# Routed experts: token rows carry their residual, number and weight, each expert scatters its finished rows to the output, and the row loads are cut into 96 and 11 partitions

## The chip, the cores and the metric

The kernel runs on one core of a Trainium2 chip. The metric is the device time of one execution in microseconds (us). A core has a matrix engine (TensorE, PE in the rows; its weight loads are PEld), a vector engine (VectorE, DVE), a scalar engine (ScalarE, ACT), GpSimd (POOL) and SyncE (SP), each with its own instruction stream. They meet through semaphores, and data moves between the chip's memory and the on-chip memory through 16 DMA engines. A DMA is issued by an instruction on some engine's queue; here SP issues the plain loads and stores, and POOL the indirect ones, whose row addresses come from a tile of indices.

## The reference

Six layers on 2048 tokens (32 batches of 64) of 256 values. The change touches the last one, a feed-forward layer with eight experts, and the end of the layer before it:

```python
capacity = int(N / E * 1.25) + 1            # 2048 / 8 * 1.25 + 1 = 321
logits = xf @ wg
scores = softmax(logits)
top1 = argmax(scores)                       # the expert of each token
combine_w = scores[top1]
rank = cumsum(one_hot(top1), axis=0)[top1] - 1
valid = rank < capacity
slot = where(valid, top1 * capacity + rank, trash)
buf = zeros(...).at[slot].set(xf)           # xf: the normalised tokens, by expert
h = gelu(buf[e] @ W1[e] + b1[e])            # 321 x 256 -> 321 x 1024
y = h @ W2[e] + b2[e]                       # -> 321 x 256
out = x + where(valid, y[slot], 0) * combine_w
```

Everything is float32.

## The kernel before, in words

`perceiver` calls six stages one after the other. Between two stages all engines meet at a barrier, and each stage has its own tiles and semaphores. The change is in the last two.

**The Laplacian attention and router** (`laplacian_attention_and_router`, line 2059) works on 8 groups of 256 tokens: two streams, four rounds of a loop. For each group SP loads the residual and the attention of the stage before (L2130, L2131), and stores `x4` (the residual that the expert layer adds to, L2141), `xn` (its layer norm, the experts' input, L2145) and the router's logits (L2149). SP issues what belongs to one group in the order in which it is made. Loads are issued one round ahead. The two groups' steps alternate by `in_turn`. The tile `b.y4` may be written again once the stores of the round before have landed, which DVE checks by the semaphore `out` against 48 r (three stores of 16 each). At the start of this stage POOL clears a zero tile (L2162), and when the first layer norm is done it stores zeros over the whole of `buf` with four DMAs (L2167). `buf` is 8 x 321 = 2568 rows of 256 values in the chip's memory, 321 rows for each expert.

**The routed experts** (`routed_experts`, line 2305) has these parts:

1. *Routing.* SP loads the logits, four constants, `xn` into the tile `xs` (L2375), the weights of experts 0 and 1 (L2361 to L2363: 1 MB, 1 MB and a bias row broadcast to 128 partitions), and `x4` into `x4s` (L2378). DVE computes each token's expert and rank (L2476 to L2512) and gives two index tiles: `put` (where the token's row goes in `buf`) and `get` (where its result will stand in `ybuf`). PE helps with two products for the counts (L2424, L2425).
2. *Scatter.* POOL waits for `xs` and the indices and writes the 2048 rows of `xn` to `buf` with 16 indirect DMAs of 128 rows (L2458).
3. *Experts.* SP waits until all 16 have landed, loads the rows of experts 0 and 1 into `xe` (L2381) and then issues the weights of experts 2 to 5 (six sets of weight buffers, `NW`). An expert's 321 rows stand on 107 partitions, three rows on each, so the load is a transfer of 107 partitions of 3072 B. `xe` has two buffers. In its loop SP waits until expert e has been transposed, loads the rows of e + 2 (L2389), waits for the result `ye` and stores it to `ybuf` (L2391, 107 partitions again), and then loads the weights of e + 6.
   PE does for each expert: six transposes of `xe` (L2433), wait for ScalarE's copy `xeT` (L2409), 16 products for the hidden layer (L2441; each shows as two records), wait for the last of the eight Gelus (L2414), and 24 products for the output (L2447). DVE adds the bias from PSUM into `ye` (L2521, L2522).
4. *Combining.* POOL waits until all of `ybuf` has landed (L2462) and reads the 2048 result rows back in token order with 16 indirect DMAs (L2464). DVE multiplies each by its weight and adds `x4s` (L2530), and SP stores the output in four DMAs of 512 tokens (L2398).

`rows_of(b, e)` (line 2355) gives the rows of expert e as 107 partitions of three rows. `Chain.step` makes DVE wait for its own instruction.

Of the kernel before, what the change touches and what calls it, by code (L numbers as in the profile page):

```python
# [20 lines left out]
TOK = 128  # L21
# [2028 lines left out]

ERF_P = (-2.72614225801306e-10, 2.77068142495902e-08, -2.10102402082508e-06, -5.69250639462346e-05,
# [7 lines left out]
def laplacian_attention_and_router(nc, consts, x2, oT, W, x4, xn, logits, buf):  # L2059
# [6 lines left out]
    E = W["wg"].shape[1]  # L2066
    with ExitStack() as ctx:
# [15 lines left out]
        zeros = m.sbuf("zeros", [ROWS, 6 * 256])  # L2083
# [42 lines left out]
        def _(sp):  # L2126
# [6 lines left out]
            def work(b, r, more):  # L2133
# [7 lines left out]
                sp.dma_start(tiles_of(x4, 2 * r + b.number), b.y4[:]).then_inc(b.sem("out"), 16)  # L2141
                yield
# [13 lines left out]
            for b in streams:  # L2156
                sp.wait_ge(b.sem("out"), 48 * R)

        @block.gpsimd
        def _(pool):  # L2160

            nc.gpsimd.memset(zeros[:], 0.0).then_inc(sem("zeros"), 1)  # L2162
            pool.wait_ge(sem("zeros"), 1)
            pool.wait_ge(streams[0].sem("a_norm"), 1)
            slots = buf.rearrange("(a p t) n -> a p (t n)", p=ROWS, t=6)
            for a in range(buf.shape[0] // (6 * ROWS)):
                pool.dma_start(slots[a], zeros[:]).then_inc(sem("zeroed"), 16)  # L2167
            pool.wait_ge(sem("zeroed"), 16 * (buf.shape[0] // (6 * ROWS)))

        @block.scalar  # L2170
        def _(act):
            act.wait_ge(sem("const_in"), NL)
            def work(b, r):
# [21 lines left out]
                act.wait_ge(b.sem("out"), 48 * r)  # L2195
# [44 lines left out]
        def _(dve):  # L2240
# [12 lines left out]
            def work(b, r):  # L2253
# [37 lines left out]
                dve.wait_ge(b.sem("out"), 48 * r)  # L2291
# [13 lines left out]
def routed_experts(nc, consts, x4, xn, logits, W, buf, ybuf, out):  # L2305
# [9 lines left out]
    FAR = 100000.0  # L2315
    NW = 6
    assert TE * ROWS == CAP
    with ExitStack() as ctx:
# [6 lines left out]
        xs = m.sbuf("xs", [TOK, NT, D])  # L2325
        x4s = m.sbuf("x4s", [TOK, NT, D])
# [14 lines left out]
        get = m.sbuf("get", [TOK, NT], U32)  # L2341
# [4 lines left out]
        xe = m.sbuf("xe", [ROWS, 2, TE, D])  # L2346
# [24 lines left out]
        def _(sp):  # L2371
            sp.dma_start(lg[:], logits.rearrange("(t p) e -> p t e", p=TOK)).then_inc(sem("lg_in"), 16)
            for dst, src in ((ident[:], consts["ident"]), (upto[:], consts["upto"]), (order[:], consts["order"]), (b1[:], W["b1"])):
# [22 lines left out]
            for t in range(0, NT, 4):  # L2396
                sp.wait_ge(sem("mix"), t // 4 + 1)
                sp.dma_start(out[TOK * t:TOK * t + 4 * TOK, :].rearrange("(t p) n -> p t n", p=TOK), x4s[:, t:t + 4]).then_inc(sem("out"), 16)  # L2398
            sp.wait_ge(sem("out"), 16 * (NT // 4))

        @block.scalar
        def _(act):
            act.wait_ge(sem("shifted"), 1)
            nc.scalar.activation(ex[:], ex[:], ACT.Exp).then_inc(sem("exp"), 1)
            act.wait_ge(sem("const_in"), 64)

            def expert(e, par):
                act.wait_ge(sem("xT_ps"), e + 1)
                nc.scalar.activation(xeT[:, par], pX[:, :, 0:CAP], ACT.Copy).then_inc(sem("xT"), 1)  # L2409
                if e:  # L2410
                    act.wait_ge(sem("y_ps"), e)
                for f in range(NFT):
                    act.wait_ge(sem("h_ps"), e * NFT + f + 1)
                    nc.scalar.activation(hT[:, f, :], pH[:, f % 4, 0:CAP], ACT.Gelu, bias=b1[:, bass.ds(e, 1), f:f + 1].rearrange("p a b -> p (a b)")).then_inc(sem("h"), 1)  # L2414
            for e in range(E):
                expert(e, e % 2)

        @block.tensor
        def _(pe):
            pe.wait_ge(sem("const_in"), 64)  # L2420
# [7 lines left out]
            def expert(e):  # L2428
                i, par, at = e // 2, e % 2, e % NW
                pe.wait_ge(sem(f"xe_in{par}"), 16 * (i + 1))  # L2430
                for k in range(2):
                    for t in range(TE):
                        o = nc.tensor.transpose(pX[:, k, ROWS * t:ROWS * t + ROWS], xe[:, par, t, 128 * k:128 * k + 128], ident[0:ROWS, 0:ROWS])  # L2433
                o.then_inc(sem("xT_ps"), 1)
                pe.wait_ge(sem("xT"), e + 1)
                weights_here(pe, e)
                for f in range(NFT):
# [4 lines left out]
                    o.then_inc(sem("h_ps"), 1)  # L2442
                pe.wait_ge(sem("h"), (e + 1) * NFT)
                pe.wait_ge(sem("ye"), e)
# [3 lines left out]
                o.then_inc(sem("y_ps"), 1)  # L2448
            for e in range(E):
# [3 lines left out]
        def _(pool):  # L2453
            nc.gpsimd.memset(ones[:], 1.0).then_inc(sem("set"), 1)
            pool.wait_ge(sem("xs_in"), 16)
            pool.wait_ge(sem("slots"), 1)
            for t in range(NT):
                pool.indirect_dma_start(buf, bass.IndirectOffsetOnAxis(put[:, t:t + 1], 0), xs[:, t, :], None,  # L2458
                                        bounds_check=SLOTS - 1, oob_is_err=False).then_inc(sem("put"), 16)
            pool.wait_ge(sem("put"), 16 * NT)  # L2460
            for par in range(2):
                pool.wait_ge(sem(f"ye_out{par}"), 8 * E)  # L2462
            for t in range(NT):
                pool.indirect_dma_start(xs[:, t, :], None, ybuf, bass.IndirectOffsetOnAxis(get[:, t:t + 1], 0),  # L2464
                                        bounds_check=SLOTS - 1, oob_is_err=False).then_inc(sem(f"got{t // 4}"), 16)

        @block.vector
        def _(dve):
# [5 lines left out]

            dve.wait_ge(sem("lg_in"), 16)
# [4 lines left out]
            dve.wait_ge(sem("const_in"), 64)  # L2480
# [27 lines left out]
            chain.step(v.tensor_scalar(get[:], slot[:], float(SLOTS - 1), None, ALU.min))  # L2508
            chain.step(v.tensor_tensor(weight[:], weight[:], room[:], ALU.mult))
# [5 lines left out]
            def expert(e):  # L2515
                i, par, at = e // 2, e % 2, e % NW
                dve.wait_ge(sem("y_ps"), e + 1)
                weights_here(dve, e)
                if i:
                    dve.wait_ge(sem(f"ye_out{par}"), 16 * i)  # L2520
                v.tensor_tensor(ye[:, par, 0:2], pY[0:ROWS, 0, :].rearrange("p (t n) -> p t n", n=D), b2[0:ROWS, at].unsqueeze(1).to_broadcast([ROWS, 2, D]), ALU.add)  # L2521
                v.tensor_tensor(ye[:, par, 2], pY[0:ROWS, 1, 0:D], b2[0:ROWS, at], ALU.add).then_inc(sem("ye"), 1)  # L2522
            for e in range(E):
                expert(e)

            dve.wait_ge(sem("x4_in"), 16)
# [21 lines left out]
def shape_constants(latents=64, experts=8, buckets=32):  # L2548
# [81 lines left out]
```

## Time and profile before

| | us |
|---|---|
| median of 3 runs | 3820.42 (3816.07 to 3820.52) |
| the profiled execution's own time | 3818.75 |
| its span in the trace | 3817.0 |
| PE busy in the span | 3019.8 (79%) |
| DVE busy | 2548.8 (67%) |
| ACT busy | 1931.1 (51%) |
| POOL busy | 748.6 (20%) |
| start of the Laplacian stage (its first load) | 3286.09 |
| start of the expert stage (its first load) | 3503.85 |

The profile is of one execution. Times of instructions are counted from the start of the span. A row of the timeline has the start, the duration, the engine, the line of the kernel and the operation with what it writes and reads; "x48" is the number of records merged into the row, and the brackets say how long the engine had been idle and what ended that. "PEclk" is the granted TensorE clock as a share of 2.4 GHz, so 0.50 is the lower level, 1.2 GHz. "DMA" is the mean busy share of the 16 DMA engines, so that one engine alone gives 0.06.

### The profile page before, as it was taken

To read this page: it belongs to the slowest core of one execution; us is meant where nothing else is said; L and a number is where in the kernel's file an instruction comes from. 1 tells how busy PE (TensorE), PEld (TensorE's weight loads), DVE (VectorE), ACT (ScalarE), POOL (GpSimd) and SP (SyncE) were. 2 spreads that over 40 slices of the span, in tenths; PEclk is the share of its full clock that TensorE was granted. 3 is DMA by queue.
4 is the path that set the end of the run, shared out by engine and by line. 5 is a ranking of instruction groups with operands and counts; after the bars stand their busy time and mean duration, and the time that the engine had idled before them with its cause. 6 is when DMAs were issued, how large, how long until landed. Compare 5 with 4: busy or idle time off the path is not lost. (4 is left out here: it accounts for less than half of the span.)

```text
span 3817.0 us, 103916 instructions
## 1 busy us (share of the span) xinstructions
PE 3019.8 (79%) x36990; PEld 2570.1 (67%) x36990; DVE 2548.8 (67%) x7485; ACT 1931.1 (51%) x4178; POOL 748.6 (20%) x836
## 2 busy tenths in 40 slices
PE   3449999999999985566379999999999999543674
PEld 3348888888888884444258788787888888432453
DVE  5568888888888854766567777776777777464000
ACT  1146666667666643333236666666666666321111
POOL 0223233332333310000132211211221221001001
PEclk7669999999999996777569999999999999765887
DMA  2123332323323302000111111111111111213411
GB/s 65 52 85 81 82 83 81 81 82 82 83 81 80 84 10 66 23 22 17 37 33 40 42 42 40 42 40 39 43 39 43 43 39 27 77 41 111 156 48 61
DMA packets 235455, 221.58 MB, mean 58 GB/s; under 512 B 69516, under 2 KB 228545, under 8 KB 234816
## 3 DMA queue, kind: packets, MB, share of 16 engines
q1 hardware_dynamic: 232896, 208.22, 19.4%
q0 software_dynamic: 2048, 6.68, 0.5%
q8 instruction: 304, 4.98, 0.5%
q14 instruction: 207, 1.70, 0.1%
HBM read 186.30 MB, written 28.39 MB: 56 GB/s over the span
## 5 line engine op out<-in xcount | busy, mean ns | idle before, releaser
L1867 ACT ACTIVATE xb_P<-xb_sc 124x1024 f32<-124x1024 f32 (+1 forms) x416 | 405.6, 1023 | 428.9 <-PE xb_sc L1959 428.9
L2029 DVE CUSTOM_DVE_ANT_0 xb_junk<-xb_ring,xb_mbias 128x372 bf16<-128x372 f32 (+2 forms) x1024 | 526.3, 571 | 102.9 <-PE xb_ring L1936 98.6
L1936 PE MATMUL xb_ring<-xb_khi,xb_qhi 32*128 32x372 f32 (+2 forms) x1024 | 405.5, 443 | 45.4 <-DVE xb_kf L2014 16.0
L879 PE MATMUL xa_acc<-xa_raw,xa_P 124*128 124x193 f32 x1664 | 315.6, 330 | 7.3 <-ACT xa_P L754 7.0
L1959 PE MATMUL xb_sc<-xb_qs,xb_kf 32*124 32x128 f32 x6656 | 317.3, 271 | 0.0
L2014 DVE COPY xb_kf<-xb_ring 128x372 f32<-128x372 f32 (+2 forms) x256 | 138.8, 572 | 244.8 <-ACT xb_khi L1831 239.8
L1907 PE MATMUL xb_ring<-xb_xst,xb_whi 128*128 128x372 f32 (+2 forms) x768 | 263.2, 370 | 43.6 <-DVE xb_xst L2008 38.0
L1907 PE MATMUL xb_ring<-xb_whi,xb_xst 128*124 128x256 f32 (+1 forms) x1248 | 286.4, 292 | 2.9 <-DVE xb_maxes L2029 0.4
L1936 PEld LDWEIGHTS xb_ring<-xb_khi,xb_qhi 32*128 32x128 f32 x1024 | 181.3, 185 | 153.1 <-DVE xb_maxes L2029 56.4
L1959 PEld LDWEIGHTS xb_sc<-xb_qs,xb_kf 32*124 32x124 f32 x6656 | 282.7, 182 | 0.0
L879 PEld LDWEIGHTS xa_acc<-xa_raw,xa_P 124*128 124x128 f32 x1664 | 266.4, 189 | 18.7 <-ACT xa_P L754 12.3
L1804 POOL TENSOR_SCALAR xb_augk<-xb_mask,xb_some 1x1602 bf16<-1x1602 uint8 x128 | 206.4, 1613 | 252.6 <-PE xb_sc L1959 236.0
L865 PE MATMUL xa_sc<-xa_qblk,xa_kT 128*124 128x128 f32 x1664 | 239.0, 272 | 0.0
L1976 PE MATMUL xb_acc<-xb_P,xb_val 124*17 124x64 f32 x13312 | 230.8, 220 | 4.2 <-ACT xb_P L1867 4.2
L1907 PEld LDWEIGHTS xb_ring<-xb_whi,xb_xst 128*124 128x124 f32 (+1 forms) x1248 | 216.8, 188 | 22.7 <-DVE xb_maxes L2029 15.9
L672 POOL CAST xa_kTr<-xa_kT 128x744 fp32r<-128x744 f32 (+1 forms) x128 | 109.9, 858 | 621.2 <-ACT xa_kT L740 621.2
L1976 PEld LDWEIGHTS xb_acc<-xb_P,xb_val 124*17 124x17 f32 x13312 | 190.7, 97 | 44.0 <-issue 15.7
L1907 PE MATMUL xb_ring<-xb_wlo,xb_xst 128*124 128x256 f32 (+1 forms) x832 | 218.3, 284 | 0.0
L865 PEld LDWEIGHTS xa_sc<-xa_qblk,xa_kT 128*124 128x124 f32 x1664 | 216.1, 187 | 0.1
L1956 PE MATMUL xb_sc<-xb_augq,xb_augk 32*124 32x256 bf16 (+1 forms) x1664 | 201.3, 303 | 1.6 <-ACT xb_P L1867 1.6
L1907 PEld LDWEIGHTS xb_ring<-xb_xst,xb_whi 128*128 128x128 f32 x768 | 146.5, 193 | 76.7 <-issue 43.0
L1907 PE MATMUL xb_ring<-xb_xst,xb_wlo 128*128 128x372 f32 (+2 forms) x512 | 180.2, 352 | 0.0
(430 smaller groups left out, 7720.8 us busy)
## 6 DMA issues: line engine op xcount, KB each, us to landing
xa_raw<-in_ctx SPq DMA_DIRECT2D x64, 279.0 KB
ex_w<-in_W SPq DMA_DIRECT2D x16, 1024.0 KB, 10.1
xa_raw<-in_ctx SPq DMA_DIRECT2D x32, 372.0 KB
xa_xTr<-in_ctxT SPq DMA_DIRECT2D x64, 186.0 KB, 2.5
xb_raw<-in_ctxT SPq DMA_DIRECT2D x64, 186.0 KB, 2.5
xa_xTr<-in_ctxT SPq DMA_DIRECT2D x32, 248.0 KB, 2.7
xb_raw<-in_ctxT SPq DMA_DIRECT2D x32, 248.0 KB
xa_mask<-in_mask SPq DMA_DIRECT2D x32, 200.1 KB, 5.3
```

The source lines that it names most:

```text
L672: nc.gpsimd.tensor_copy(kTr[:, c % 2, :, 0:W], kT[:, p, :, k0:k0 + W]).then_inc(sem("kTr"), 1)
L865: i = nc.tensor.matmul(s_[0:w, 256 * u + 128 * o:256 * u + 128 * o + 128], kt[:, o, :], qblk[:, t3, o, :], start=False, stop=True, skip_gr ...
L879: i = nc.tensor.matmul(acc[:, o, :], w, raw[0:KEYS, t3, t, :], start=t == 0 and o == 0, stop=t == NKT - 1, skip_group_check=True)
L1804: nc.gpsimd.tensor_scalar(augk[r:r + 1, p, :], mask8[r:r + 1, :], -1.0, some[r:r + 1, 1:2], ALU.add, ALU.mult).then_inc(sem("augk"), 1)
L1867: nc.scalar.activation(P[0:w, pbuf(t, p), :].rearrange("p (r n) -> p r n", r=4), sc[0:w, :, half], ACT.Exp).then_inc(sem("exped"), 1)
L1907: i = nc.tensor.matmul(out, l, r, start=k == 0, stop=k == 4)
L1936: i = nc.tensor.matmul(bank[:, 0:w], qhi[r, p, o, 128 * s:128 * s + 128], khi[r, p, o, k0:k0 + w], start=True, stop=True)
L1956: nc.tensor.matmul(sc[0:w, r, at:at + 256], augk[rows(r), p, keys], augq[rows(r), p, :], start=True, stop=True)
L1959: i = nc.tensor.matmul(sc[0:w, r, at + 128 * o:at + 128 * o + 128], kf[rows(r), p, o, keys], qs[rows(r), p, o, 128 * (r % 2):128 * (r % 2) ...
L1976: i = nc.tensor.matmul(acc[32 * j:32 * j + VW, 64 * g:64 * g + 64], val[0:w, p, c, h, :], P[0:w, pbuf(c, p), place(h):place(h) + 64], star ...
L2014: v.tensor_copy(kf[:, p, o, k0:k0 + w], ring[f % 3][:, 0:w]).then_inc(sem("kf"), 1)
L2029: v.tensor_tensor_reduce(out=junk[:, k, 0:w], in0=ring[f % 3][:, 0:w], in1=mbias[:, p, k0:k0 + w], scale=1.0, scalar=-3.0e38, op0=ALU.add, ...
```

## The change

In the Laplacian stage:

- `x4` of each group is stored a second time, to `out`. The semaphore is counted against 64 r.
- `buf` has rows of 528 values (2112 B): 256 of `xn`, 256 of `x4`, and 16 more of which two are used. It is cleared as a flat tensor with 9 DMAs of 128 partitions and 1177 values, from a tile of that size.

In the expert stage:

- One tile `row` (128 x 16 x 528) takes the place of `xs` and `x4s`. It is loaded in four DMAs: `xn` and `x4` for the first eight tiles of tokens, then for the last eight. DVE clears the last 16 columns, and puts in the token's number (from a new constant, counted from 1) and its weight.
- The scatter's first eight DMAs wait for the first half of `row`, the others for the second.
- `xe` has four buffers (`NX`) of 528 values a row. The load of an expert's rows is two DMAs, of partitions 0 to 95 and 96 to 106, now 6336 B on each partition. Four experts are loaded at once after the scatter; the rows of e + 4 are loaded when `ye` of expert e is done.
- PE transposes the rows of expert e + 1 (`turn`) between the hidden and the output products of expert e, and ScalarE copies them (`turned`) after the Gelus of e.
- After the bias, DVE makes the output's row numbers (`to`; a row without a token gets a number beyond the bound) and computes weight times result plus residual in three instructions. PE waits for `biased`, not for `ye`.
- POOL scatters the three rows of each partition to `out` with three indirect DMAs of 107 rows for each expert. `ybuf`, the read back, DVE's combining pass and the four stores are gone.

```diff
+EXTRA = 16
@@ laplacian_attention_and_router
+    SHARE = buf.shape[0] * buf.shape[1] // 128
+    SIZE = next(k for k in range(3000, 0, -1) if SHARE % k == 0)
-        zeros = m.sbuf("zeros", [ROWS, 6 * 256])
+        zeros = m.sbuf("zeros", [128, SIZE])
                 sp.dma_start(tiles_of(x4, 2 * r + b.number), b.y4[:]).then_inc(b.sem("out"), 16)
+                sp.dma_start(tiles_of(out, 2 * r + b.number), b.y4[:]).then_inc(b.sem("out"), 16)
-            slots = buf.rearrange("(a p t) n -> a p (t n)", p=ROWS, t=6)
-            for a in range(buf.shape[0] // (6 * ROWS)):
-                pool.dma_start(slots[a], zeros[:]).then_inc(sem("zeroed"), 16)
+            flat = buf.rearrange("s n -> (s n)").rearrange("(p q) -> p q", p=128)
+            for k in range(0, SHARE, SIZE):
+                pool.dma_start(flat[:, k:k + SIZE], zeros[:]).then_inc(sem("zeroed"), 16)
@@ routed_experts
+    WIDE = 2 * D + EXTRA
     NW = 6
+    NX = 4
+    EVEN = 96
-        xe = m.sbuf("xe", [ROWS, 2, TE, D])
+        xe = m.sbuf("xe", [ROWS, NX, TE, WIDE])
+        def in_two(a):
+            return a[0:EVEN], a[EVEN:ROWS]
+        def tokens_in(sp, e):
+            for to, of in zip(in_two(xe[:, e % NX]), in_two(rows_of(buf, e))):
+                sp.dma_start(to, of).then_inc(sem(f"xe_in{e % NX}"), 16)
@@ sync
-            sp.dma_start(xs[:], xn.rearrange("(t p) n -> p t n", p=TOK)).then_inc(sem("xs_in"), 16)
+            for h in range(2):
+                for k, part in enumerate((xn, x4)):
+                    tiles = slice(NT // 2 * h, NT // 2 * h + NT // 2)
+                    sp.dma_start(row[:, tiles, D * k:D * k + D], part.rearrange("(t p) n -> p t n", p=TOK)[:, tiles]).then_inc(sem(f"row_in{h}"), 16)
             for e in range(2):
                 weights_in(sp, e)
-            sp.dma_start(x4s[:], x4.rearrange("(t p) n -> p t n", p=TOK)).then_inc(sem("x4_in"), 16)
             sp.wait_ge(sem("put"), 16 * NT)
-            for e in range(2):
-                sp.dma_start(xe[:, e], rows_of(buf, e)).then_inc(sem(f"xe_in{e}"), 16)
+            for e in range(NX):
+                tokens_in(sp, e)
             for e in range(2, NW):
                 weights_in(sp, e)
             def expert(e):
-                par = e % 2
-                if e + 2 < E:
-                    sp.wait_ge(sem("xT_ps"), e + 1)
-                    sp.dma_start(xe[:, par], rows_of(buf, e + 2)).then_inc(sem(f"xe_in{par}"), 16)
-                sp.wait_ge(sem("ye"), e + 1)
-                sp.dma_start(rows_of(ybuf, e), ye[:, par]).then_inc(sem(f"ye_out{par}"), 16)
+                if e + NX < E:
+                    sp.wait_ge(sem("ye"), e + 1)
+                    tokens_in(sp, e + NX)
                 if e + NW < E:
+                    sp.wait_ge(sem("y_ps"), e + 1)
+                    sp.wait_ge(sem("biased"), e + 1)
                     weights_in(sp, e + NW)
@@ tensor
                 for f in range(NFT):
                     ...
                     o.then_inc(sem("h_ps"), 1)
+                if e + 1 < E:
+                    turn(e + 1)
                 pe.wait_ge(sem("h"), (e + 1) * NFT)
-                pe.wait_ge(sem("ye"), e)
+                pe.wait_ge(sem("biased"), e)
@@ gpsimd
             for t in range(NT):
+                if t % (NT // 2) == 0:
+                    pool.wait_ge(sem(f"row_in{t // (NT // 2)}"), 32)
-                pool.indirect_dma_start(buf, bass.IndirectOffsetOnAxis(put[:, t:t + 1], 0), xs[:, t, :], None,
+                pool.indirect_dma_start(buf, bass.IndirectOffsetOnAxis(put[:, t:t + 1], 0), row[:, t, :], None,
                                         bounds_check=SLOTS - 1, oob_is_err=False).then_inc(sem("put"), 16)
             pool.wait_ge(sem("put"), 16 * NT)
+            for e in range(E):
+                par = e % 2
+                pool.wait_ge(sem("ye"), e + 1)
+                for t in range(TE):
+                    pool.indirect_dma_start(out, bass.IndirectOffsetOnAxis(to[:, par, t:t + 1], 0), ye[:, par, t, :], None,
+                                            bounds_check=N - 1, oob_is_err=False).then_inc(sem(f"out{par}"), 16)
-            for t in range(NT):
-                pool.indirect_dma_start(xs[:, t, :], None, ybuf, bass.IndirectOffsetOnAxis(get[:, t:t + 1], 0),
-                                        bounds_check=SLOTS - 1, oob_is_err=False).then_inc(sem(f"got{t // 4}"), 16)
@@ vector
+            chain.step(v.memset(row[:, :, 2 * D:WIDE], 0.0))
-            chain.step(v.tensor_scalar(get[:], slot[:], float(SLOTS - 1), None, ALU.min))
-            chain.step(v.tensor_tensor(weight[:], weight[:], room[:], ALU.mult))
+            v.tensor_copy(row[:, :, 2 * D], number[:])
+            v.tensor_tensor(row[:, :, 2 * D + 1], weight[:], room[:], ALU.mult)
                 if i:
-                    dve.wait_ge(sem(f"ye_out{par}"), 16 * i)
+                    dve.wait_ge(sem(f"out{par}"), 16 * TE * i)
                 v.tensor_tensor(ye[:, par, 0:2], pY[...] + b2)
-                v.tensor_tensor(ye[:, par, 2], pY[...] + b2).then_inc(sem("ye"), 1)
+                v.tensor_tensor(ye[:, par, 2], pY[...] + b2).then_inc(sem("biased"), 1)
+                chain.step(v.tensor_scalar(gone[:, par], xe[:, at_x, :, 2 * D], 0.5, FAR, ALU.is_le, ALU.mult))
+                v.scalar_tensor_tensor(out=to[:, par], in0=xe[:, at_x, :, 2 * D], scalar=-1.0, in1=gone[:, par], op0=ALU.add, op1=ALU.add)
+                dve.wait_ge(sem("biased"), e + 1)
+                for t in range(TE):
+                    o = v.scalar_tensor_tensor(out=ye[:, par, t], in0=ye[:, par, t], scalar=xe[:, at_x, t, 2 * D + 1:2 * D + 2], in1=xe[:, at_x, t, D:2 * D], op0=ALU.mult, op1=ALU.add)
+                o.then_inc(sem("ye"), 1)
-            for t in range(NT):
-                if t % 4 == 0:
-                    dve.wait_ge(sem(f"got{t // 4}"), 64)
-                i = v.scalar_tensor_tensor(out=x4s[:, t, :], in0=xs[:, t, :], scalar=weight[:, t:t + 1], in1=x4s[:, t, :], op0=ALU.mult, op1=ALU.add)
```

## Rows read from the trace of the kernel before

**Rows 1.** The page: the span, and the chain that ended last, by line
```profile
span 3817.0 us, 103916 instructions
...
DMA ex_xe<-buf 2%; SPq L2361 1%; SPq L2363 1%; SPq L2391 1%; PE ex_pH L2441 1%; PE ex_pY L2447 1%; DMA ybuf<-ex_ye 0%; POOL buf L2458 0%; POOL ex_xs L2464 0%; DMA ex_xs<-xn 0%; SPq L2362 0%; DMA ex_xs<-ybuf,ex_get 0%; SPq L2381 0%; DMA buf<-ex_xs,ex_put 0%; SPq L2374 0%
```

**Rows 2.** Timeline of PE in the expert stage
```profile
3553.80 1.31 PE L2433 MATMUL ex_pX<-ex_ident,ex_xe 107*128 107x107 f32 x6 [43.32 <-DMA ex_xe<-buf]
3555.96 11.38 PE L2441 MATMUL ex_pH<-ex_xeT,ex_w 128*128 128x321 f32 x32 [0.86 <-ACT ex_xeT L2409]
3567.96 10.61 PE L2447 MATMUL ex_pY<-ex_w,ex_hT 128*107 128x256 f32 x48 [0.62 <-ACT ex_hT L2414]
3578.41 0.71 PE L2433 MATMUL ex_pX<-ex_ident,ex_xe 107*128 107x107 f32 x6
3579.91 8.92 PE L2441 MATMUL ex_pH<-ex_xeT,ex_w 128*128 128x321 f32 x32 [0.79 <-ACT ex_xeT L2409]
...
3638.52 1.33 PE L2433 MATMUL ex_pX<-ex_ident,ex_xe 107*128 107x107 f32 x6 [7.74 <-DMA ex_xe<-buf]
...
3697.13 10.61 PE L2441 MATMUL ex_pH<-ex_xeT,ex_w 128*128 128x321 f32 x32 [0.80 <-ACT ex_xeT L2409]
```

**Rows 3.** Busy time by stretch (us; records in brackets), granted clock, DMA share, GB/s
```profile
3538.50:3553.80 15.30, 0.01 (x1) 0.04 (x1) 0.00 (x0) 0.00 (x0) 0.00 (x0) 0.50 0.06 23
...
3578.40:3589.40 11.00, 9.64 (x39) 6.48 (x37) 1.02 (x2) 4.93 (x9) 0.00 (x0) 1.00 0.95 323
...
3698.50:3701.50 3.00, 3.00 (x8) 1.97 (x7) 0.00 (x0) 0.75 (x2) 0.00 (x0) 0.60 0.06 26
```

**Rows 4.** Timeline of SP's queue in the expert stage
```profile
3542.49 12.43 SPq L2361 DMA_DIRECT2D ex_w<-in_W  x1
...
3586.95 0.53 SPq L2389 DMA_DIRECT2D ex_xe<-buf  x1
```

**Rows 5.** DMA view, 3538.5 to 3553.8: issues, KB each, us to landing
```profile
ex_w<-in_W SPq DMA_DIRECT2D x1, 1024.0 KB, 20.0
```

**Rows 6.** Chain of waits through the routing and the scatter: start, us, what
```profile
3506.81 8.49 DMA ex_xs<-xn
...
3535.59 2.89 DMA buf<-ex_xs,ex_put
```

**Rows 7.** Tile `ex_xs`: duration ns min/median/max, first and last start us
```profile
L2458 POOL DMA_INDIRECT buf<-ex_xs,ex_put x16: 980/981/1085, 3516.2 to 3535.6; - x16
L2464 POOL DMA_INDIRECT ex_xs<-ybuf,ex_get x16: 994/998/1260, 3787.3 to 3807.3; - x16
L2530 DVE SCALAR_TENSOR_TENSOR ex_x4s<-ex_xs,ex_weight,ex_x4s x16: 472/478/486, 3794.1 to 3812.5; 128x256 f32<-128x256 f32 x16
...
DMA to landing us min/median/max: 2.7/2.8/4.1
```

**Rows 8.** Timeline of DVE in the routing: the index tile
```profile
3514.90 0.18 DVE L2510 TENSOR_TENSOR ex_put<-ex_slot,ex_far 128x16 uint32<-128x16 f32 x1
```

**Rows 9.** DMA view, 3508 to 3538: packets, and POOL's queue (packets, MB, share)
```profile
DMA packets 7801, 10.60 MB, mean 353 GB/s; under 512 B 392, under 2 KB 6806, under 8 KB 7801
...
q0 software_dynamic: 768, 1.95, 17.3%
```

**Rows 10.** Tile `ex_ye`: DVE's first bias instruction
```profile
L2521 DVE TENSOR_TENSOR ex_ye<-ex_pY,ex_b x8: 691/691/693, 3578.7 to 3770.1; 107x512 f32<-107x512 f32 x8
```

**Rows 11.** Chain of waits at the end of the experts: start, us, what
```profile
3771.18 15.23 DMA ybuf<-ex_ye
```

**Rows 12.** Line 2398, the stores of the output
```profile
L2398 SPq DMA_DIRECT2D out<-ex_x4s x4: 372/386/400, 3795.8 to 3813.0; - x4
...
DMA to landing us min/median/max: 2.9/3.2/3.6
```

**Rows 13.** The Laplacian stage: clearing on POOL's queue, DMA view 3300 to 3345
```profile
q0 software_dynamic: 512, 2.63, 18.0%
```

**Rows 14.** Waits of SP's queue, 3310 to 3500 (us in total, times, longest)
```profile
SPq L56 <- DVE la_y L2292: 125.0, 8, 36.1
```

More of the change, by code:

```diff
@@ L2302, in _, with routed_experts @@
                 b.chain.leave(R, PER)
-def routed_experts(nc, consts, x4, xn, logits, W, buf, ybuf, out):
+def routed_experts(nc, consts, x4, xn, logits, W, buf, out):
     N, D = x4.shape
@@ L2324, in routed_experts @@
         order = m.sbuf("order", [128, E])
-        xs = m.sbuf("xs", [TOK, NT, D])
-        x4s = m.sbuf("x4s", [TOK, NT, D])
+        row = m.sbuf("row", [TOK, NT, WIDE])
+        number = m.sbuf("number", [TOK, NT])
         lg = m.sbuf("lg", [TOK, NT, E])
@@ L2340, in routed_experts @@
         put = m.sbuf("put", [TOK, NT], U32)
-        get = m.sbuf("get", [TOK, NT], U32)
+        gone = m.sbuf("gone", [ROWS, 2, TE])
+        to = m.sbuf("to", [ROWS, 2, TE], U32)
         w1 = m.sbuf("w1", [128, NW, 2, F])
@@ L2395, in _ @@
                 expert(e)
[L2396 to L2399, printed above, removed]
         @block.scalar
@@ L2414, in expert @@
                     nc.scalar.activation(hT[:, f, :], pH[:, f % 4, 0:CAP], ACT.Gelu, bias=b1[:, bass.ds(e, 1), f:f + 1].rearrange("p a b -> p (a b)")).then_inc(sem("h"), 1)
+            turned(0)
             for e in range(E):
-                expert(e, e % 2)
+                expert(e)
+                if e + 1 < E:
+                    turned(e + 1)
         @block.tensor
         def _(pe):
-            pe.wait_ge(sem("const_in"), 64)
+            pe.wait_ge(sem("const_in"), 80)
             pe.wait_ge(sem("oh"), 1)
@@ L2426, in _, with turn, expert @@
             pe.wait_ge(sem("ranked"), 1)
-            def expert(e):
-                i, par, at = e // 2, e % 2, e % NW
-                pe.wait_ge(sem(f"xe_in{par}"), 16 * (i + 1))
+            def turn(e):
+                pe.wait_ge(sem(f"xe_in{e % NX}"), 32 * (e // NX + 1))
                 for k in range(2):
                     for t in range(TE):
-                        o = nc.tensor.transpose(pX[:, k, ROWS * t:ROWS * t + ROWS], xe[:, par, t, 128 * k:128 * k + 128], ident[0:ROWS, 0:ROWS])
+                        o = nc.tensor.transpose(pX[:, k, ROWS * t:ROWS * t + ROWS], xe[:, e % NX, t, 128 * k:128 * k + 128], ident[0:ROWS, 0:ROWS])
                 o.then_inc(sem("xT_ps"), 1)
+            def expert(e):
+                par, at = e % 2, e % NW
                 pe.wait_ge(sem("xT"), e + 1)
@@ L2545, in relative_buckets, with shape_constants @@
     return np.where(n < exact, n, np.minimum(far, buckets - 1))
-def shape_constants(latents=64, experts=8, buckets=32):
+def shape_constants(latents=64, experts=8, tokens=2048, buckets=32):
     i = np.arange(128)
@@ L2560, in shape_constants @@
         "sel": (i[:, None] == i[None] // 32 * 32 + 16).astype(np.float32),
+        "number": (i[:, None] + 128 * np.arange(tokens // 128)[None] + 1).astype(np.float32),
         "order": np.tile(experts - np.arange(experts, dtype=np.float32), (128, 1)),
@@ L2575, in perceiver @@
     logits = scratch("logits", (N, E))
-    buf, ybuf = scratch("buf", (slots, D)), scratch("ybuf", (slots, D))
+    buf = scratch("buf", (slots, 2 * D + EXTRA))
     latent_projections(nc, a, a["x"], a["ln_l_g"], a["ln_l_b"], a["qn_g"], a["kn_g"], a["WqT"], a["WlkvT"], qT, klT, vl)
@@ L2581, in perceiver @@
     wide_cross_attention(nc, a, a["ctxT"], a["mask1"], a["Wkv3"], q3T, oT3)
-    laplacian_attention_and_router(nc, a, x2, oT3, a, x4, xn, logits, buf)
-    routed_experts(nc, a, x4, xn, logits, a, buf, ybuf, out)
+    laplacian_attention_and_router(nc, a, x2, oT3, a, x4, xn, logits, buf, out)
+    routed_experts(nc, a, x4, xn, logits, a, buf, out)
 def layout(i):
```

34 lines of the change are left out of this document (17 added, 17 removed).

## The prediction

> **What bounds the kernel now.** I read the page first. Only the last stages are touched, and the chain that ended last runs through the expert stage alone: loads of `xe`, SP's issues, the two products of PE, the store to `ybuf`, POOL's two sets of indirect DMAs [rows 1]. So I read that stage in order of time.
>
> PE's timeline shows one chain per expert: transposes, copy, hidden products, last Gelu, output products [rows 2]. PE starts at 3553.80, after 43 us of waiting for the first rows. Between experts it waits again, 7.74 us ahead of expert 3 and less ahead of others [rows 2]. The last output product ends at 3770.1, when the bias begins [rows 10]. That is 216.3 us for eight experts, and 3817.0 - 3770.1 = 46.9 us are left behind them.
>
> The stretches tell why. From 3538.5 to 3553.8 nothing but the first loads of rows runs, with a DMA share of 0.06 and 23 GB/s: one engine of 16 [rows 3]. A load of 107 x 3072 B = 329 KB takes 15.3 us so. Beside it SP's queue is clogged: one weight load takes 12.43 us to issue, so that SP reaches the rows of expert 2 only at 3586.95 [rows 4].
>
> The granted clock matters too. Where PE ran through, it was 1.00 (2.4 GHz) and 16 hidden products took 8.92 us; behind a stop of some 2.5 us it fell to 0.50 (1.2 GHz) for a while, with 0.60 as the mean of the first full stretch, and they took 10.61 [rows 2, 3].
>
> **Part 1: up to the first transpose.** *Row loads.* Before, 2 MB of `xn` landed at 3506.81 + 8.49 = 3515.30 [rows 6], just behind the indices, ready at 3515.1 [rows 8]. Now the first half of `row` is 2 MB too, one small constant and one issue later: 3516.2, +0.9 us. DVE's routing loses two short steps and gains two: zero.
>
> *Scatter.* POOL issues one DMA each (3535.6 - 3516.2) / 15 = 1.293 us, of which 0.98 is the instruction [rows 7]. The rows are now 2112 B, not 1024. Bounds: the time goes by rows (+0), or by bytes (0.98 x 1.06 x 16 = +16.6 us). I take +0: the instruction writes one address per row, and gather and scatter of 128 rows cost the same 0.98 to 1.00 [rows 7].
>
> *DMA traffic.* From 3508 to 3538, 10.60 MB moved at 353 GB/s, 1.95 MB of it the scatter's [rows 9]. After the change the loads are the same (`row` 4.2 MB, two sets of weights 4.5 MB), the scatter is 2048 x 2112 B = 4.3 MB: 13.0 MB in all, at about 365 GB/s until 3543.5. The two queues share: POOL's needs 270 KB each 1.293 us, 208 GB/s, which leaves 157 for the second half of `row` (2.1 MB, 13.4 us, lands at about 3529.5). POOL wants it at 3516.9 + 8 x 1.293 = 3527, so a stall of 2.5 us; the last scatter is issued near 3539.5 and lands 2.9 us later by its row [rows 6]: 3542.4 instead of 3538.5.
>
> *First rows.* Expert 0's load is now 107 x 6336 B = 678 KB, 96 partitions of it over 16 engines, behind some 0.5 MB of weights still queued: 1.2 MB at 365 GB/s is 3.2 us, and about 0.9 us of start and completion: 3546.5. Bounds: 3543 (no stall, no backlog), and 3555 (traffic at 300 GB/s, 13.0 MB until 3551, then 4 us). **PE starts 7.3 us earlier** (-11 to +1).
>
> A weight load of 1 MB, 3 us at 353 GB/s, took 20.0 us to land when issued behind the one-engine loads [rows 5]: an engine works through SP's transfers in the order of issue. The Trainium skill (DMA: Bandwidth & Descriptors, Queues, rings and completion order) states that each engine consumes a queue's ring in order; this trace agrees. If the rows passed the weights instead, the sum would be 1.4 us less.
>
> **Part 2: the experts.** Per expert PE has left: hidden products 8.92 at the full clock, transposes of the next expert 0.77, output products 10.61 [rows 2]. The last Gelu, 0.62 us of waiting before, lies beside the transposes; the copy, 0.80 before, beside the output products. About 0.1 for waits already met: 20.4 us. The rows of experts 0 to 3 (2.7 MB) and the weights of 2 to 5 (8.9 MB) need 33 us at 353 GB/s, so all are there by 3580; expert 2 is due at 3592. Later an expert needs 2.2 + 0.7 + 0.3 MB in 20.4 us, 160 GB/s. POOL's three scatters, 3.9 us, and DVE's 3 us per expert fit beside it, and PE waits only for the bias of the expert before, 9 us old by then.
>
> Expert 0: 1.31 + 0.85 + 11.38 (clock still low) + 0.77 + 10.61 + 0.1 = 25.0. Experts 1 to 6: 6 x 20.4 = 122.4. Expert 7 has no next one, so it pays the Gelu: 8.92 + 0.62 + 10.61 + 0.05 = 20.2. Together 167.6 instead of 216.3: **-48.7 us**. Bounds: 0.3 less per expert (-51), or the low clock at each start (1.7 x 7 = 12 us more: -37).
>
> **Part 3: the end.** After the last product: bias 1.05 (3770.1 to the store at 3771.18) [rows 10, 11], two tiny steps 0.4, three combining instructions at most 0.48 each, 1.3 [rows 7]; POOL 0.9 to begin (3515.30 to 3516.2) [rows 6, 7] and 3 x 0.98 + 2 x 0.31 = 3.6; landing 2.9 [rows 6]; closing 0.8 (the last store was issued at 3813.0 and landed by 3816.2) [rows 12]. Sum 10.9 instead of 46.9: **-36.0 us**. Gone are the store to `ybuf` (15.23 us on one engine [rows 11]), 16 read-backs of 1.3 us, their combining, the last store. Bounds -38 and -32 (POOL slower beside DVE, a scatter of 107 rows landing in 5).
>
> **Part 4: the Laplacian stage.** SP issues 8 more stores of 0.4 us; it waited 125 us for DVE there [rows 14]. Clearing goes from 2.63 MB, which took 18.0% of 45 us, 8.1 us of all engines, to 5.42 MB, 8.6 us more [rows 13]; it begins near 3309 and ends near 3335, while the loads for the next round are due at about 3354. I take 0. The cover is one round of prefetch; without it the cost would be up to 9 us. Below nothing: -0.3, a smaller clear.
>
> **Sum**: -7.3 - 48.7 - 36.0 + 0 = -92.0. The profiled execution took 3818.75, 1.7 below the median of 3820.42, so 3726.8 against its own time and 3728 against the median: 3727.
>
> **Rivals.**
>
> *A. The scatter or its traffic is dearer* (part 1's upper bounds): POOL's time grows with the bytes, 0 to 16.6 us, or the traffic's rate falls. For it: the engines were at a share near 1 from 3508 on, with 353 GB/s already [rows 9]. Against: equal time for reads and writes. Gives 3735 to 3744. Chance 0.14.
>
> *B. The clock still falls* between experts: +12, 3739. For it: a stop of 2.5 us was enough [rows 2, 3]. Against: what is left between products is 0.1 us, and expert 1, with a stop of 0.8, ran at 1.00. Chance 0.06.
>
> *C. Slower: the cut does not spread the load*, so the change does not do what it says, and the rows, now of twice the bytes, still go through one engine. At 26 GB/s, the best that one engine shows [rows 3], 678 KB are 26.1 us, and that engine's sixteenth of a weight set 5.3 us. Eight loads and the six sets queued among them are 8 x 26.1 + 6 x 5.3 = 241 us from 3542: the last rows land at 3783. Behind them stand 0.8 + 10.6 + 8.9 + 0.6 + 10.6 = 31.5 us of PE and 10.9 of the end: 3825 in span, +8, time 3828 (at 23 GB/s, 3859). It decides from 20.4 us a load for the experts' pace, and from about 25 us a load for slower than before. For it: one engine is what the rows show of such loads, and four now stand ahead of the weights. Against: traffic with the weights' 128 partitions reached 323 GB/s [rows 3]. Chance 0.03. The Trainium skill (DMA: Bandwidth & Descriptors, Why a DMA increments its semaphore by 16 and not by 1) has the number of engines as the largest up to 16 that divides the outer sizes of both sides: 1 for 107, as seen here, 16 for 96 and 11 for 11. By that rule C does not happen.
>
> *D. The Laplacian stage pays* for its second store and its clear, 3 to 9 us: 3730 to 3736. Chance 0.10.
>
> **How the numbers follow.** The forecast has 0.67, rivals A 0.14, D 0.10, B 0.06, C 0.03. The forecast's own range is 3718 to 3736 by its bounds. The range reaches to A and B: 3717 to 3746. A measurement of this kernel can tell 0.2%, 8 us, from no change: faster 0.96, same 0.01, slower 0.03.
>
> **What would show it.** PE starts near 3546; its hidden products take 8.9 us from expert 1 on, with transposes between them and the output products and no idle over 0.2 us; the granted clock is 1.00 from expert 1 to 7; after the scatter the DMA share is near 1, not 0.06; SP never issues a row load late; the last output product ends near 3714 and the span 11 us later. I am wrong if row loads show 25 GB/s, if POOL's scatters take longer than 1.3 us, if PE waits for `xe` or `biased`, or if the expert stage starts later than 3504.

## The result and the profile after

The changed kernel takes 3734.88 us (median of 4 runs, 3732.13 to 3735.89), against 3820.47 of the kernel before beside it: a ratio of 0.9778, with a 95% interval of 0.9761 to 0.9794. That is 85.6 us less; 93 were forecast, and the time lies in the range given. The profiled execution has a span of 3733.4 us, against 3817.0 before.

The page of the changed kernel, against [rows 1]. The loads of `xe` no longer lead the chain that ended last; the two products of PE do:

```profile
span 3733.4 us, 103978 instructions
...
PE ex_pY L2471 2%; PE ex_pH L2463 2%; DMA ex_row<-x 0%; POOL buf L2484 0%; DMA buf<-ex_row,ex_put 0%; POOL out L2491 0%; DMA ex_xe<-buf 0%; ACT ex_hT L2431 0%; SPq L2392 0%; SPq L2396 0%; PE ex_pX L2452 0%; DVE ex_ye L2558 0%; ACT ex_xeT L2424 0%; DVE ex_ye L2552 0%; DVEq L2327 0%
```

PE's timeline in the expert stage, against [rows 2] (start us, duration, engine, line, operation, records, and in brackets the idle time before and what ended it):

```profile
3553.28 1.30 PE L2452 MATMUL ex_pX<-ex_ident,ex_xe 107*128 107x107 f32 x6 [36.72 <-DMA ex_xe<-buf]
3555.45 11.03 PE L2463 MATMUL ex_pH<-ex_xeT,ex_w 128*128 128x321 f32 x32 [0.86 <-ACT ex_xeT L2424]
3566.32 0.71 PE L2452 MATMUL ex_pX<-ex_ident,ex_xe 107*128 107x107 f32 x6
3567.10 10.61 PE L2471 MATMUL ex_pY<-ex_w,ex_hT 128*107 128x256 f32 x48
3577.54 8.82 PE L2463 MATMUL ex_pH<-ex_xeT,ex_w 128*128 128x321 f32 x32
3586.20 0.71 PE L2452 MATMUL ex_pX<-ex_ident,ex_xe 107*128 107x107 f32 x6
...
3597.43 8.82 PE L2463 MATMUL ex_pH<-ex_xeT,ex_w 128*128 128x321 f32 x32
...
3706.27 10.61 PE L2471 MATMUL ex_pY<-ex_w,ex_hT 128*107 128x256 f32 x48 [0.62 <-ACT ex_hT L2431]
```

After expert 0's own start (the wait for its rows, and 0.86 us for their copy) no row has a wait but the last, which is expert 7's for its Gelu. An expert takes 3597.43 - 3577.54 = 19.9 us. The stretches say the same, against [rows 3] (busy us and records of PE, PEld, DVE, ACT, POOL; granted clock, DMA share, GB/s; the share adds up the times of the packets, so it can come out a little above 1):

```profile
3532.00:3540.00 8.00, 0.00 (x0) 0.00 (x0) 0.00 (x0) 0.00 (x0) 6.17 (x7) 0.50 1.05 406
...
3548.30:3551.30 3.00, 0.00 (x0) 0.00 (x0) 0.00 (x0) 0.00 (x0) 0.00 (x0) 0.50 0.83 224
...
3548.00:3556.00 8.00, 1.85 (x7) 1.50 (x8) 0.00 (x0) 1.29 (x2) 0.00 (x0) 0.50 0.91 215
...
3597.40:3716.90 119.50, 118.53 (x511) 88.69 (x510) 14.66 (x42) 28.88 (x53) 41.04 (x18) 1.00 0.23 52
```

The row loads now use nearly all of the 16 engines: the share is 0.83 in the 3 us before the next weights are issued, and 0.91 over the 8 us, where one load had 0.06. PE is busy for 118.53 of 119.50 us with the clock at 1.00. SP's queue is not clogged any more, against [rows 4]: the eight row loads (two for each of four experts) take 3.52 us to issue.

```profile
3547.82 3.52 SPq L2375 DMA_DIRECT2D ex_xe<-buf  x8
```

What the scatter into `buf` and the first row load wait for shows in the chain of waits (start, us, what), against [rows 6]; the scatter's last DMA now lands 5.86 us after its start, where 2.89 were seen:

```profile
3515.48 12.29 DMA ex_row<-x
...
3541.94 5.86 DMA buf<-ex_row,ex_put
...
3548.21 4.94 DMA ex_xe<-buf
```

The scatters to the output, by the tiles `ex_to` and, for the first scatter, `ex_row` (duration ns min/median/max, first and last start us), against [rows 7]. The 16 wide scatters cost 0.97 us each, as the narrow ones did; the 24 new ones cost 2.28:

```profile
L2491 POOL DMA_INDIRECT out<-ex_ye,ex_to x24: 2272/2280/2307, 3581.4 to 3725.8; - x24
...
DMA to landing us min/median/max: 5.8/8.0/13.0
```
```profile
L2484 POOL DMA_INDIRECT buf<-ex_row,ex_put x16: 967/972/1059, 3522.7 to 3541.9; - x16
```

I cut the expert stage of every kernel in three, from its first load (the logits): **A** until PE's first transpose, **B** until the last output product ends, **C** until the end of the span. S is the start of the stage. All are us of the profiled execution.

| kernel | S | A | B | C | median of the runs |
|---|---|---|---|---|---|
| before | 3503.9 | 49.9 | 216.3 | 46.9 | 3820.4 |
| changed | 3509.4 | 43.9 | 163.6 | 16.5 | 3734.9 |
| row load uncut | 3506.3 | 66.0 | 265.6 | 16.6 | 3856.4 |
| before, with the cut only | 3508.5 | 37.4 | 174.7 | 34.3 | 3754.3 |
| transposes in the old place | 3507.1 | 43.8 | 175.0 | 16.6 | 3743.1 |
| scatter to `out` of 128 rows | 3508.6 | 43.5 | 163.8 | 12.5 | 3727.5 |
| scatter to `out` of 112 rows | 3504.8 | 43.8 | 163.6 | 12.5 | 3726.6 (one run) |
| weights of expert 1 late | 3506.7 | 40.7 | 163.5 | 16.6 | 3728.9 |
| 128 rows and weights late | 3505.9 | 40.9 | 163.4 | 12.5 | 3725.5 |
| the same, by thirds | 3511.1 | 40.8 | 163.4 | 8.4 | 3724.0 |

S is the time of the stages before. It moved by up to 6 us between the eight kernels that have the changed kernel's code there (3504.8 to 3511.1), which is what blurs the medians; A, B and C repeat within a few tenths where nothing in them was touched. So the small differences of runs 3 to 8 from the changed kernel are read from A, B and C: by the medians alone none is clear, since the intervals of their ratios overlap that of the changed kernel, 0.9761 to 0.9794 (run 5 is a single one).

### The profile page after: what moved, and what is told of

The parts are those of the page before. It is cut to its first block and busy times, and to the rows that moved or that the text cites. A ratio compares the mean times of both kernels' runs of the same rounds, so it can differ in the third digit from the quotient of the medians.

```text
span 3733.4 us, 103978 instructions
## 1 busy us (share of the span) xinstructions
PE 3021.3 (81%) x36990; PEld 2577.0 (69%) x36990; DVE 2553.5 (68%) x7510; ACT 1931.4 (52%) x4178; POOL 788.9 (21%) x849
## 3 DMA queue, kind: packets, MB, share of 16 engines
q0 software_dynamic: 13328, 11.56, 1.0%
## 5 line engine op out<-in xcount | busy, mean ns | idle before, releaser
L1907 PE MATMUL xb_ring<-xb_xst,xb_whi 128*128 128x372 f32 (+2 forms) x768 | 262.8, 369 | 43.8 <-DVE xb_xst L2008 38.0
```

The lines of the kernel that those rows point to most:

```text
L1907: i = nc.tensor.matmul(out, l, r, start=k == 0, stop=k == 4)
```

## The experiments

Each ratio is to the kernel before as it was measured beside that run: 3818.35 us for runs 1, 3, 4 and 5, and 3817.67 for the others.

**1. The cut taken back in the changed kernel.**

```diff
-            return a[0:EVEN], a[EVEN:ROWS]
+            return (a,)
```

(and PE waits for 16, not 32, per load.)

> The changed kernel, but the rows of an expert are one load of 107 partitions again (still 6336 B on each). Theory (a transfer of 107 partitions goes through one DMA engine, and the cut is what lets the four-deep loads work): 678 KB at 23 to 26 GB/s are 26 to 29.5 us a load, more than the 19.9 us that PE needs for an expert, so the expert stage is bound by one engine: DMA share near 0.06 for most of it, PE waiting for ex_xe before most experts, last output product 90 to 125 us later than in the changed kernel, time 3825 to 3860, slower than the kernel before. Rival (with four buffers the loads are far enough ahead, the cut is worth only the first load): time 3755 to 3765, PE waits only before expert 0.

Measured: 3856.44 us, ratio to before 1.0098 (1.0083 to 1.0114). PE's timeline and one stretch of this kernel:

```profile
3572.23 1.30 PE L2452 MATMUL ex_pX<-ex_ident,ex_xe 107*128 107x107 f32 x6 [58.82 <-DMA ex_xe<-buf]
...
3598.14 1.33 PE L2452 MATMUL ex_pX<-ex_ident,ex_xe 107*128 107x107 f32 x6 [11.83 <-DMA ex_xe<-buf]
...
3624.94 1.33 PE L2452 MATMUL ex_pX<-ex_ident,ex_xe 107*128 107x107 f32 x6 [3.97 <-DMA ex_xe<-buf]
...
3661.48 11.03 PE L2463 MATMUL ex_pH<-ex_xeT,ex_w 128*128 128x321 f32 x32 [23.79 <-DMA ex_b<-in_b]
...
3709.01 1.33 PE L2452 MATMUL ex_pX<-ex_ident,ex_xe 107*128 107x107 f32 x6 [16.61 <-DMA ex_xe<-buf]
...
3804.60 1.33 PE L2452 MATMUL ex_pX<-ex_ident,ex_xe 107*128 107x107 f32 x6 [5.14 <-DMA ex_xe<-buf]
```
```profile
3550.00:3600.00 50.00, 15.08 (x46) 10.41 (x47) 0.00 (x0) 6.71 (x11) 0.00 (x0) 0.60 0.06 27
```

The theory holds. While only row loads run, the share is 0.06. PE waits for rows before six of the seven later experts, and once for 23.8 us for the weights of expert 2, which were issued behind four row loads. Without its cut the change is a loss of 38 us: it doubled the bytes of a load and put four in a row, more than the one engine could carry beside PE.

This was the forecast's slower rival, priced at 3828 with 26 GB/s and at 3859 with 23. The rate was the first one: the rows of experts 0 to 2 are there at 3572.23, 3598.14 and 3624.94, so 678 KB took 26 us, which is 26 GB/s. The span, 3854.4, is still 29 us above that price's 3825. The first load was issued 3 us later than priced (3544.63). From there to the last rows it took 260 us, not 241. Behind them it took 49.8, not 42.4, of which 5.7 are the longer end that the changed kernel has too.

**2. The cut alone, in the kernel before.**

```diff
-                sp.dma_start(xe[:, e], rows_of(buf, e)).then_inc(sem(f"xe_in{e}"), 16)
+                for a, b in cut:
+                    sp.dma_start(xe[a:b, e], rows_of(buf, e)[a:b]).then_inc(sem(f"xe_in{e}"), 16)
```

with `cut = ((0, 96), (96, ROWS))`, the same at the other load of `xe` and at the store to `ybuf`, and the waits counted double.

> The kernel before, with one edit: the loads of xe and the stores to ybuf are each cut into partitions 0 to 95 and 96 to 106. Theory (most of the gain of the whole change is the one DMA engine that carried every row): expert 0 starts about 11 us earlier, the experts run at the 21.5 us of the run with the transposes in their old place (175 instead of 216 us), the last store lands in 3 instead of 15 us: 64 us in all, time near 3756. Rival (the loads are mostly hidden, and the gain comes from the scatter to the output and the new order): only the first load and the last store shrink, 23 us, time near 3797.

Measured: 3754.33 us, ratio 0.9833 (0.9818 to 0.9848). PE's timeline of this kernel, where no wait for rows is left after the first:

```profile
3545.88 1.30 PE L2438 MATMUL ex_pX<-ex_ident,ex_xe 107*128 107x107 f32 x6 [30.83 <-DMA ex_xe<-buf]
...
3591.46 0.72 PE L2438 MATMUL ex_pX<-ex_ident,ex_xe 107*128 107x107 f32 x6
3592.97 8.92 PE L2446 MATMUL ex_pH<-ex_xeT,ex_w 128*128 128x321 f32 x32 [0.80 <-ACT ex_xeT L2414]
```
```profile
3550.00:3720.00 170.00, 159.49 (x678) 117.58 (x677) 7.16 (x14) 38.74 (x71) 0.00 (x0) 0.99 0.30 96
```

63 of the 86 us come with the cut: A falls by 12.5, B by 41.6, C by 12.6. B's share is the waits for rows, and the clock that now stays up: 0.99 over the 170 us. Beside this kernel, the rest of the change costs 6.5 us in A, gives 11.1 in B and 17.8 in C. The 6.5 are 1.0 for a later first scatter, 3.4 for the later landing of the last one, and 2.1 for the larger row load.

**3. The transposes in their old place.**

```diff
-                if e + 1 < E:
-                    turn(e + 1)
...
             for e in range(E):
+                turn(e)
                 expert(e)
```

and the same on ScalarE.

> The changed kernel, but PE transposes the rows of expert e just before its hidden products, and ScalarE copies them there, as in the kernel before. Theory (the new order hides 0.80 us of copy and 0.62 us of Gelu per expert, and the gaps are too short for the clock to fall): a period of 8.8 + 0.62 + 10.6 + 0.71 + 0.80 = 21.5 us instead of 19.9, +11.7 us over seven experts, granted clock 1.00 in the experts 1 to 7, time near 3746.5. Rival (the stop of 1.5 us between experts is enough to lower the clock, so that the new order is worth the clock too): hidden products 10.6 instead of 8.8 us, +24 us, time near 3759.

Measured: 3743.08 us, ratio 0.9795 (0.9780 to 0.9810). PE's timeline of this kernel:

```profile
3596.70 0.72 PE L2450 MATMUL ex_pX<-ex_ident,ex_xe 107*128 107x107 f32 x6
3598.21 8.92 PE L2461 MATMUL ex_pH<-ex_xeT,ex_w 128*128 128x321 f32 x32 [0.80 <-ACT ex_xeT L2424]
3607.75 10.61 PE L2467 MATMUL ex_pY<-ex_w,ex_hT 128*107 128x256 f32 x48 [0.62 <-ACT ex_hT L2431]
```

A period of 21.5 us with the hidden products at 8.92: the theory. The clock did not fall over the 0.80 us of waiting, so the new order is worth its two gaps and no more: 11.4 us in B, 8.2 between the medians. The time is 3.4 us below the expected 3746.5; S is 2.3 us earlier than in the changed kernel.

**4 and 5. The scatter to the output with 128 and with 112 rows.** `ye` and `to` get more partitions, the added ones hold a number beyond the bound:

```diff
-        to = m.sbuf("to", [ROWS, 2, TE], U32)
+        to = m.sbuf("to", [128, 2, TE], U32)
-        ye = m.sbuf("ye", [ROWS, 2, TE, D])
+        ye = m.sbuf("ye", [128, 2, TE, D])
...
+            v.memset(ye[:], 0.0)
+            chain.step(v.memset(to[:], int(FAR)))
```

> The changed kernel, but ye and its row numbers have 128 partitions: partitions 107 to 127 are cleared once and hold a number beyond the bound, so that each scatter to out has 128 rows, 21 more of them beyond the bound. Theory (107 is a prime, so the indirect DMA is cut into many small packets on one engine; that is why it takes 2.28 us and lands after 5.8): 0.98 us each as for the 128 rows of the first scatter, landing near 3 us; the tail behind the last output product falls from 16.5 to 9 to 10 us, time 3727 to 3729. Rival 1 (rows beyond the bound cost the extra time): more of them, so 2.3 us or more and no gain, 3735 or later. Rival 2 (writing rows of 1 KB to scattered places of out is slow in itself): 2.3 us or more, 3735 or later.

> As the kernel with 128 partitions, but with 112, the next multiple of 16 above 107, so only 5 rows more lie beyond the bound. Theory (the divisor decides): about 0.9 us a scatter and a landing near 3 us, as with 128. Rival (the number of rows counts, or only a power of two is fast): near 2 us each and a landing above 5 us.

Measured: 3727.51 us with 128 (ratio 0.9759, 0.9746 to 0.9773), 3726.58 with 112 (one run). The tile `ex_to` of the two kernels, 128 first:

```profile
L2491 POOL DMA_INDIRECT out<-ex_ye,ex_to x24: 969/974/981, 3580.2 to 3721.8; - x24
```
```profile
L2491 POOL DMA_INDIRECT out<-ex_ye,ex_to x24: 935/942/959, 3576.6 to 3718.1; - x24
```

Five rows more make an indirect DMA 2.4 times faster, and rows beyond the bound cost little: 0.97 us with 21 of them, 0.94 with 5. So it is the count of 107. The trace's packets agree: POOL's queue had 10,752 packets behind the first scatters in the changed kernel, most of them of 16 bytes; over the whole run its packets fall from 13,328 to 3,728 with 112 or 128 rows. That is 448 packets for each scatter to `out` against 48. Why 107 rows are cut so is not shown. That 112 and 128 are multiples of 16 and 107 is a prime makes a rule by divisors likely, as with the loads, but no other count was tried.

C fell by 4.0, which is the issue of three scatters, 3 x 1.3. The faster landing gave nothing: the end is 12.5 us, where 9 to 10 were expected. That the time came out as expected all the same is luck: of the 7.4 us between the medians C has 4.0, and the rest is none of the edit's doing that the trace shows. The records of POOL's own stream behind the last scatter, in us from its end, tell why:

```
                      wait for the landing over   drain at the stage's end   end of the span
changed (107 rows)    +3.6                        0.54 long                  +5.4
128 rows              +1.3                        3.31 long                  +5.7
```

At the end of the stage POOL has an instruction that drains the engine, and the wait and the drain together end the span 5.4 to 5.7 us after its last indirect DMA, however early that lands. The kernel before has this drain too. There it ended at 3812.65, 4.2 us after the last gather, but DVE's combining and the last store went on until 3816.1, so it cost nothing.

**6. The weights of expert 1 behind the row loads.**

```diff
-            for e in range(2):
-                weights_in(sp, e)
+            weights_in(sp, 0)
             sp.wait_ge(sem("put"), 16 * NT)
             for e in range(NX):
                 tokens_in(sp, e)
-            for e in range(2, NW):
+            for e in range(1, NW):
                 weights_in(sp, e)
```

> The changed kernel, but the weights of expert 1 are issued behind the row loads instead of before the scatter: 2.2 of 13 MB less ahead of it. Theory (DMA traffic delays the second half of row, the landing of the last scatter and the first row load): last scatter lands after about 3 instead of 5.9 us, the first rows 3.5 instead of 5.3 us behind it, time 3730 to 3731. Rival (POOL's issue of 16 x 1.28 us sets the time, traffic does not): no change, 3735.

Measured: 3728.85 us, ratio 0.9769 (0.9755 to 0.9782). The chain of waits of this kernel:

```profile
3539.25 2.66 DMA buf<-ex_row,ex_put
...
3542.32 4.89 DMA ex_xe<-buf
```

Half of the theory: the last scatter lands after 2.66 instead of 5.86 us, and A falls by 3.2. The first rows still take 4.9 us, as before, where 3.5 were expected, though hardly anything was queued ahead of them. So that part is the load itself, not a backlog. The median fell by 6.0 us, and 2.7 of that is an earlier S.

**7 and 8. Both edits, and then the last expert by thirds.** In the last kernel PE signals the output products twice:

```diff
-                o.then_inc(sem("y_ps"), 1)
+                    if t:
+                        o.then_inc(sem("y_ps"), 1)
```

and DVE and POOL handle t = 0 and 1 while PE computes t = 2.

> The two edits together: 128 partitions in the scatter to out, and the weights of expert 1 behind the row loads. If both theories hold and they do not meet, their gains add: about 4 us at the tail against the changed kernel (as the 128 partitions gave in their trace) and about 4.5 us before the experts, time 3723 to 3726. If the issue of POOL sets the time before the experts, 3727 to 3730.

> As the kernel with both edits, and PE signals the first two thirds of the output products (t = 0 and 1) on their own, so that DVE biases and combines them and POOL scatters them while PE computes the third. Theory (the tail is a chain of DVE 2.6 us, POOL 0.8 + 3 x 1.28 us and 5.5 us of closing): only one bias, one combining step and one scatter are left behind the last product, the tail falls from 12.5 to about 8.5 us, time 3719 to 3722. Rival (the closing after POOL's last DMA is what counts and grows when more is behind it): no change against the kernel with both edits.

Measured: 3725.54 us (ratio 0.9764, 0.9750 to 0.9777) and 3723.97 us (0.9752, 0.9738 to 0.9765). The gains of the two edits add in the trace: A 40.9, C 12.5. The thirds take C to 8.4, by 4.1 as expected. In the medians only 1.6 shows, the two intervals overlap, and the time is above the expected 3719 to 3722; the last kernel's profile had an S that was 5.2 us later, with the same code there. The last kernel has the lowest median, 11 us under the changed one, and its tail is down to one combining step, one scatter and the closing. POOL's timeline of it, whose last row starts 6.6 us before the end of its span, 3723.6:

```profile
3716.97 0.97 POOL L2492 DMA_INDIRECT out<-ex_ye,ex_to  x1 [0.39 <-issue]
```

## Why the prediction was right, and where it was off

The sum was -92.0 us of span, the profile has -83.6. The mechanism was the one forecast: with the cut the row loads ran on nearly all engines, PE's waits went, the clock stayed up, and the end became short. What was off are the sizes of terms. Term by term:

**Up to the first transpose: -7.3 forecast, -6.1 found** (A). The row loads landed as forecast: POOL waited 13.1 us and began 13.3 us after the start of the stage (12.3 before). The wide scatter goes by rows, not bytes: 0.97 us each, so the lower bound was right. The last scatter landed 38.4 us after the start of the stage, forecast 38.5, but that is luck, for two errors cancelled. The stall of 2.5 us was not there: the second half of `row` landed at 3527.77, 18.4 us after the start where 25.7 were forecast, and the ninth scatter, the first that reads it, ran at 3533.00. The forecast had given the loads only what the scatters left of the rate; they got more of it. The last landing took 5.86 us instead of 2.9, with the traffic still at 373 to 406 GB/s; run 6 shows that this was the traffic. The first rows then took 5.3 us, not 4.1. I had put 3.2 us of that down to 1.2 MB at full rate. Run 6 shows that with the backlog gone the load's piece of the chain is still 4.89 us, against 4.94.

The rule weighed there (the Trainium skill, DMA: Bandwidth & Descriptors, Queues, rings and completion order: an engine takes a queue's transfers in order) is borne out by run 1, where the weights of expert 2 waited behind four row loads: their last part was issued at 3637.30 and landed 24.0 us later.

**The experts: -48.7 forecast, -52.7 found** (B). Every hidden item was hidden, and rival B, the clock, did not come: 1.00 from expert 0's output products on. The period was 19.9 instead of 20.4. I had added up durations, 8.92 + 0.77 + 10.61 and 0.1; but a group's shown duration ends with its last matmul's modelled end, and the next group starts some 0.16 us before that. From start to start it is 8.66 + 0.78 + 10.45.

**The end: -36.0 forecast, -30.4 found** (C, 16.5 instead of 10.9). This is the term that was mis-sized. The step was "3 x 0.98 + 2 x 0.31 = 3.6", with the duration of a scatter of 128 rows for one of 107. It took 2.28 each (runs 4 and 5: the count 107), 3.9 us more. The rest, 1.7, is the end after POOL's last instruction: "landing 2.9 and closing 0.8" was 3.7, found 5.4. Its term for the closing was read from a kernel in which the drain of POOL was over before the last store had landed; here it stands at the very end. The 2.9 also counts from the scatter's start, so the sum had the last scatter's own 0.98 us twice; without that the closing was too short by 2.7.

**The Laplacian stage: 0 forecast, 2.1 found.** From its first load to that of the expert stage it took 217.8 us before and 219.9 after. The other kernels of this document settle what the new store and the larger clear cost. The stage's time goes with PE's mean granted clock in it, not with the code:

| code of the stage | granted clock | time of the stage |
|---|---|---|
| old (before, run 2) | 0.62 to 0.63 | 217.8, 218.1 |
| new (runs 1, 5, 8) | 0.62 to 0.63 | 217.9, 217.6, 218.0 |
| new (changed, runs 3, 4, 6, 7) | 0.59 to 0.61 | 219.3 to 219.9 |

The stretches behind three of the rows (before, changed, run 5; columns as above):

```profile
3286.09:3503.85 217.76, 99.66 (x352) 78.90 (x352) 129.50 (x364) 56.03 (x96) 3.88 (x6) 0.63 0.19 60
```
```profile
3289.51:3509.39 219.88, 103.02 (x352) 81.22 (x352) 129.45 (x364) 56.02 (x96) 6.23 (x11) 0.59 0.24 82
```
```profile
3287.24:3504.84 217.60, 99.70 (x352) 78.90 (x352) 129.49 (x364) 56.02 (x96) 6.23 (x10) 0.63 0.24 83
```

At the same clock the new code costs nothing that shows, and rival D falls. The clearing of 5.42 MB took 31.5% of 45 us, 14.2 us of all engines, and ended in the first round:

```profile
q0 software_dynamic: 1296, 5.42, 31.5%
```

Why the clock was lower in five of the eight kernels with the new code is open; only two profiles have the old code, so that the change makes it more frequent is neither shown nor excluded.

The stage began 3.4 us later than in the profile before, by what stands ahead of it, which nobody touched. These two, 5.5 us, are no term of the forecast.

Added up: +1.2 - 4.0 + 5.6 + 5.5 = 8.3, and -92.0 + 8.3 = -83.7. In the stage itself the errors of the experts and of the end, -4.0 and +5.6, nearly cancel, which is luck too.

**The signs of being wrong.** Two of those that the forecast named came. POOL's scatters to `out` took 2.28 us, over 1.3: that is the mis-sized end. The expert stage started at 3509.39, later than 3504: that is the 5.5 us above.

**The rivals.** A (a dearer scatter) was right in one point, the traffic, and it cost 3 us within A. C did not come, since the cut did spread the loads. Run 1, the change without its cut, shows what it would have cost: more than its 3828 at 26 GB/s. That 63 of the 86 us would come with the cut alone could have been read from [rows 3], but my sum cut the stage by time, not by cause, and did not say it.

## What to carry to other kernels

Look at the DMA share in the stretches where an engine waits for a load: 0.06 is one engine of 16, and the count of partitions is the first suspect. An awkward count, here 107, can be cut into a multiple of 16 and a rest; for an indirect DMA it can be padded with rows beyond the bound. Both were tried with this one count. Price an operation by a row of its own shape: 107 rows are not 128.

## What the runs showed of the hardware that was not expected

- An indirect DMA of 107 rows of 1 KB took 2.28 us on POOL, one of 112 rows 0.94, one of 128 rows 0.97, and one of 128 rows of 2112 B also 0.97.
- Behind POOL's last indirect DMA some 5.5 us pass until the span ends, with a landing after 1.3 us as with one after 3.6; a drain of up to 3.3 us fills it up.
- The first row loads moved 224 GB/s with 0.83 of the engines' time busy, which is 17 GB/s for each busy engine, where the traffic ahead of them reached 406 GB/s. It is not the width of the rows alone (6336 B on a partition): in run 1 one engine by itself moved the same rows at 26 GB/s. What makes the difference was not tried.
- TensorE kept its upper clock through waits of 0.80 us between groups, seven times in run 3. In the kernel before it had fallen behind a stop of 2.5 us with six transposes in it (3694.7 to 3697.13), and the 16 hidden products took 10.61 us instead of 8.92.
